# Expert results scattered by token, and the last layer's scores from rounded parts, in a two-layer attention and mixture-of-experts kernel

## The reference

```python
x = L0_attn_x
xn = _layernorm(x)
x = x + _L0_attn_ref(xn, ...) + _L0_ffn_ref(xn, Wg, W_in, W_out)
xn = _layernorm(x)
x = x + _L1_attn_ref(xn, key_param, ...) + _L1_ffn_ref(xn, gate_w, ...)

# _L0_attn_ref: causal attention, 16 heads of 16, 4 key heads, rotary
# _L0_ffn_ref: mixture of 8 experts with capacity C = 1280 each
top_vals, top_idx = jax.lax.top_k(softmax(xf @ Wg), 2)
loc = ...                      # place of the token in its expert's queue
keep = loc < C                 # what comes too late is dropped
gates = top_vals * keep / max(sum, 1e-09)
buf = zeros((E, C + 1, h)).at[e_flat, l_flat].set(xk)
a, g = split(einsum('ech,ehf->ecf', buf[:, :C], W_in), 2)
out_e = einsum('ecf,efh->ech', gelu(a) * g, W_out)
y = (out_pad[e_flat, l_flat].reshape(S, K, h) * gates[..., None]).sum(axis=1)

# _L1_attn_ref: queries against 32 learned patterns, sparsemax over them
scores = einsum('blhe,bshe->bhls', xn @ Wq + bq, keys)
out = einsum('bhls,bshd->blhd', sparsemax(scale * scores), values)
# _L1_ffn_ref: 8 experts and 2 shared ones, each over all tokens
```

## Time and profile before

| | us |
|---|---|
| Median of 3 runs | 2156.84 |
| Lowest and highest | 2152.84 and 2159.22 |
| The profiled execution | 2144.84 |
| Its span, first to last instruction | 2143.1 |
| TensorE busy | 1966.0 (92%) |
| VectorE busy | 1531.1 (71%) |
| ScalarE busy | 1035.6 (48%) |
| GpSimd busy | 514.3 (24%) |

### The profile page before, as it was taken

One profiled execution on the slowest core, in us unless ns is written; L12 is line 12 of the kernel. 1 busy time (PEld: TensorE's weight loads), 2 busy tenths in 40 slices (PEclk: granted clock), 3 DMA queues, 4 the chain that ended last, 5 costly groups with the idle time before them and its releaser, 6 DMA issues. The chain is left out here.

```text
span 2143.1 us, 35073 instructions
## 1 busy us (share of the span) xinstructions
PE 1966.0 (92%) x11874; PEld 1195.0 (56%) x11874; DVE 1531.1 (71%) x3473; ACT 1035.6 (48%) x2246; POOL 514.3 (24%) x932
## 2 busy tenths in 40 slices
PE   6869999999999999999799999986678999999998
PEld 3333333333333333333299999984556777777776
DVE  7879988888888888888054333325578998889883
ACT  3426677676767777777744444432331122221112
POOL 4554123322222222222233333336400000000000
PEclk9979999999999999999999999998789999999998
DMA  6555111111101111110133222215410000000005
GB/s 206 183 160 200 62 38 58 56 38 40 35 32 38 41 43 43 43 43 11 52 101 100 90 84 88 90 42 163 144 51 12 9 21 20 20 20 20 10 11 162
DMA packets 111781, 143.69 MB, mean 67 GB/s; under 512 B 12153, under 2 KB 96769, under 8 KB 111233
## 3 DMA queue, kind: packets, MB, share of 16 engines
q1 hardware_dynamic: 87248, 98.09, 14.3%
q0 software_dynamic: 10400, 31.47, 4.4%
q10 hardware_dynamic: 13968, 12.06, 1.8%
HBM read 85.10 MB, written 56.10 MB: 66 GB/s over the span
## 5 line engine op out<-in xcount | busy, mean ns | idle before, releaser
L854 ACT ACTIVATE at_wt<-at_B 128x512 f32<-128x512 f32 (+3 forms) x1280 | 607.3, 538 | 257.7 <-PE at_B L953 240.8
L1259 DVE TENSOR_REDUCE at_piece_max<-at_A 128x1 f32<-128x512 f32 x768 | 489.0, 684 | 71.3 <-PE at_A L934 61.8
L971 PE MATMUL at_O<-at_wt,at_v 128*32 128x512 f32 (+3 forms) x2560 | 313.9, 543 | 0.0
L754 POOL TENSOR_SCALAR_AFFINE_SELECT at_wt<-at_wt 128x128 f32<-128x128 f32 x512 | 147.8, 294 | 632.6 <-ACT at_wt L854 623.9
L1256 DVE CUSTOM_DVE_ANT_0 at_junk<-at_A,s_hide 128x128 bf16<-128x128 f32 (+3 forms) x512 | 230.5, 487 | 69.6 <-PE at_A L934 69.0
L1474 PE MATMUL ex_H<-ex_xT,ex_w_in 128*128 128x256 f32 x1920 | 247.8, 286 | 4.0 <-DVE ex_xT L1581 4.0
L1474 PEld LDWEIGHTS ex_H<-ex_xT,ex_w_in 128*128 128x128 f32 x1920 | 237.0, 193 | 4.4 <-DVE ex_w_out L1586 4.4
L1595 DVE TENSOR_TENSOR ex_h<-ex_act_a,ex_H 128x256 f32<-128x256 f32 x160 | 66.8, 417 | 212.7 <-ACT ex_act_a L1523 212.6
L2170 ACT ACTIVATE l_act_g<-l_G 128x512 f32<-128x512 f32 x80 | 47.9, 599 | 305.9 <-PE l_G L2084 241.3
L934 PE MATMUL at_A<-s_k,s_q 96*128 96x512 bf16 (+2 forms) x480 | 165.7, 363 | 22.3 <-PEq L104 9.6
L1516 POOL TENSOR_TENSOR ex_hT<-ex_h,ex_hT 128x256 fp32r<-128x256 f32 x160 | 123.1, 774 | 254.3 <-ACT ex_hT L1527 254.3
(11 more groups left out here) (275 smaller groups left out, 2798.9 us busy)
## 6 DMA issues: line engine op xcount, KB each, us to landing
buf<-at_room POOLq DMA_DIRECT2D x10, 1024.0 KB, 8.7
s_first_rows<-buf SPq DMA_DIRECT2D x40, 256.0 KB, 2.7
expert_out<-ex_y ACTq DMA_DIRECT2D x40, 256.0 KB, 2.2
s_raw_in<-in_W_in SPq DMA_DIRECT2D x8, 1024.0 KB
q_parts<-parts SPq DMA_DIRECT2D x16, 384.0 KB, 3.5
s_down<-in_x SPq DMA_DIRECT2D x8, 512.0 KB, 4.7
xn<-s_raw_in SPq DMA_DIRECT2D x8, 512.0 KB, 5.4
at_v<-v SPq DMA_DIRECT2D x16, 256.0 KB, 3.0
```

What stands on the lines that cost most here:

```text
L754: pool.affine_select(block_, block_, [[1, P]], ALU.is_ge, 0.0, base=0, channel_multiplier=-1).then_inc(hidden, 1)
L854: act.activation(wt[(HP * p + h) % NE_][:, q0:CH], pB_of(p, h, u)[:, q0:CH], ACT.Exp, scale=D ** -0.5).then_inc(wt_ready, 1)
L971: pe.matmul(pO[j % 2][rows, q0:CH], vs[n % 3][:, kt // TPC, kt % TPC, :], wt[(HP * p + h) % NE_][:, q0:CH], start=kt < 2 and not late, sto ...
L1259: ins = dve.tensor_reduce(top, pA[slot % NA][:, 0:w], AX.X, ALU.max)
```

## The change

Three things are changed together.

1. The experts' results. A slot's row in `buf` becomes 258 numbers long: the token's number in front, the index of its second expert behind. From these VectorE works out for each slot the row `token` or `4096 + token` (`find_target`), and GpSimd writes each step's result with two indirect DMAs of 128 rows to that row of `expert_out`, which now has 2 x 4096 rows in the order of tokens. Slots without a token carry a number beyond the bounds and are left out; `expert_out` is filled with zeros before. GpSimd does this behind the subtractions of f=1 and f=2 of the next step. `mixing` then loads `ye` with plain DMAs on SyncE.
2. The scores of the last layer. `to_scores` and the token columns are cut into two fp32r parts each, and a group takes six fp32r products instead of two float32 ones. The raw `to_scores` goes to HBM in the attention stage and comes back in mixing, where it is cut.
3. The loops of SyncE, GpSimd and VectorE in the experts and of VectorE in finish are written out. `mixed` is stored in two parts, the second over the attention output, and some semaphores are shared.

```diff
@@ attention: dispatch @@
+                if n == 0:
+                    pool.wait_ge(routing_in, 48)
+                    pool.tensor_copy(token[:, :, 1], expert[:, 1]).then_inc(token_set, 1)
+                    pool.wait_ge(token_set, 2)
...
                 for w in range(2):
-                    for c in (2 * n + w, TILES + 2 * n + w):
+                    pool.tensor_copy(xrow[n % 2][w][:, 0:E + 2:E + 1], token[:, 2 * n + w]).then_inc(token_set, 1)
+                for w in range(2):
+                    pool.wait_ge(token_set, 2 * n + w + 3)
+                    for k in range(TOPK):
+                        c = k * TILES + 2 * n + w
                         pool.indirect_dma_start(
...
+                    if n == 1 and p % 4 == 0 and p // 4 < NO_ROWS:
+                        pool.dma_start(no_rows[p // 4],
+                                       zeros[:, 1:E + 1].unsqueeze(1).to_broadcast([P, 8, E])).then_inc(buf_blank, 16)
...
+                if n == 0:
+                    sp.wait_ge(act_step, at_act["to_scores1"])
+                    sp.dma_start(d["scores_raw"], scores_raw[:]).then_inc(pats_in, 16)
@@ experts @@
-            with pool.Fori(0, ROUNDS) as j:
-                for i in range(PAIR):
-                    for f in range(FC):
-                        pool.wait_ge(h_high, FC * (PAIR * j + i) + f + 1)
-                        pool.tensor_tensor(hT[i % 2][1][:, f, :], h[i % 2][:, f, :],
-                                           hT[i % 2][0][:, f, :].bitcast(F32), ALU.subtract).then_inc(h_low, 1)
+            def store(m, t):
+                if t == 0:
+                    pool.wait_ge(target_ready, 2 * (m + 1))
+                    pool.wait_ge(y_ready, m + 1)
+                pool.indirect_dma_start(
+                    out=d["expert_out"], out_offset=bass.IndirectOffsetOnAxis(ap=target[m % 8][:, t:t + 1], axis=0),
+                    in_=y[m % 2][:, t, :], in_offset=None, bounds_check=TOPK * NT - 1, oob_is_err=False,
+                ).then_inc(y_stored[m % 2], 16)
+
+            for m in range(PAIR * ROUNDS):
+                for f in range(FC):
+                    pool.wait_ge(h_high, FC * m + f + 1)
+                    pool.tensor_tensor(hT[m % 2][1][:, f, :], h[m % 2][:, f, :],
+                                       hT[m % 2][0][:, f, :].bitcast(F32), ALU.subtract).then_inc(h_low, 1)
+                    if f in STORE_AT and m:
+                        store(m - 1, STORE_AT.index(f))
+            for t in range(RT):
+                store(PAIR * ROUNDS - 1, t)
...
-            def store(m, i):
-                act.wait_ge(y_ready, m + 1)
-                act.dma_start(one(rows_out, m), y[i][:]).then_inc(y_stored[i], 16)
...
+            def find_target(m, u):
+                dve.wait_ge(x_loaded[u % 2], 16 * (m // 2 + 1))
+                wait(dve, y_stored[u % 2], 16 * RT * (m // 2 - 3))
+                dve.tensor_scalar(second[u][:], x[u % 2][:, :, E + 1], float(m // PER), float(NT), ALU.is_equal,
+                                  ALU.mult).then_inc(target_ready, 1)
+                dve.wait_ge(target_ready, 2 * m + 1)
+                dve.tensor_tensor(target[u][:], second[u][:], x[u % 2][:, :, 0], ALU.add).then_inc(target_ready, 1)
...
+                        if f == 1 and not (last and i == PAIR - 1):
+                            find_target(m + 1, (m + 1) % 8)
@@ mixing @@
+                wait(sp, sums, SUMS * (t - NR + 1))
+                for k in range(TOPK):
+                    sp.dma_start(ye[k][t % NR][:], ye_rows[k][t]).then_inc(rows_in[t % NR], 16)
...
-        @block.gpsimd
-        def _(pool):
-            for t in range(STEPS):
-                wait(pool, sums, SUMS * (t - NR + 1))
-                for k in range(TOPK):
-                    for w in range(2):
-                        c = k * TILES + 2 * t + w
-                        pool.indirect_dma_start(
-                            out=ye[k][t % NR][:, w, :], out_offset=None, in_=d["expert_out"],
-                            in_offset=bass.IndirectOffsetOnAxis(ap=s["slot_get"][:, c:c + 1], axis=0),
-                        ).then_inc(rows_in[t % NR], 16)
...
+                if t == SPLIT_AT:
+                    act.wait_ge(raw_in, 16)
+                    act.copy(s["to_scores0"][:], scores_raw[:])
...
+                if t == SPLIT_AT + 1:
+                    dve.wait_ge(aT_ready, SPLIT_AT + 2)
+                    dve.tensor_tensor(s["to_scores1"][:], scores_raw[:], s["to_scores0"][:].bitcast(F32), ALU.subtract)
@@ layer1 @@
-                for k in range(EC):
-                    ins = pe.matmul(pZ[:], xT_score[:, k, t, :], s["to_scores"][:, k, :],
-                                    start=(k == 0), stop=(k == EC - 1))
+                steps = [(a, b, k) for a, b in TERMS for k in range(EC)]
+                for a, b, k in steps:
+                    ins = pe.matmul(pZ[:], xT_score[a][:, k, t, :], s[f"to_scores{b}"][:, k, :],
+                                    start=(a, b, k) == steps[0], stop=(a, b, k) == steps[-1])
...
-                for t in range(TPC):
-                    ins = act.copy(xT_score[:, k, t].rearrange("p (t r) -> p t r", r=16), cols[:, c % NQ * TPC + t])
-                ins.then_inc(score_cols, 1)
+                act.copy(score_view(0, k), score_rows(c, k)).then_inc(score_cols, 1)
...
+            def score_lows(c, k):
+                dve.wait_ge(score_cols, EC * c + k + 1)
+                dve.tensor_tensor(score_view(1, k), score_rows(c, k), score_view(0, k).bitcast(F32),
+                                  ALU.subtract).then_inc(score_low, 1)
...
+                    if c + 1 < NCH and i in SCORE_LOWS:
+                        score_lows(c + 1, SCORE_LOWS.index(i))
```

More of the change, by code:

```diff
@@ L533, in attention @@
         tile_count, tile_before = (scratch(KT * NX) for _ in range(2))
-        loc, within, drop, slot, slot_low, slot_put, kept = (scratch(KT) for _ in range(7))
-        FAR = float(1 << 20)
+        loc, within, drop, slot, slot_put, kept = (scratch(KT) for _ in range(6))
+        scores_raw = sb("scores_raw", [P, EC, H * NPAT])
         def half(i):
@@ L904, in _ @@
                 act.wait_ge(pe_step, at_pe[f"fold{k}"])
-                st.did(act.copy(columns(s["to_scores"][:, k], E), pQ))
+                st.did(act.copy(columns(scores_raw[:, k], E), pQ))
                 mlp_copy(4 + k)
@@ L1371, in experts @@
         y = [sb(f"y{i}", [P, RT, E]) for i in range(2)]
+        second = [sb(f"second{i}", [P, RT]) for i in range(8)]
+        target = [sb(f"target{i}", [P, RT], U32) for i in range(8)]
         over_sum = sb("over_sum", [P, TILES, H])
@@ L1452, in round_ @@
                         weights(2 * j + i // PER + 1)
-            with sp.Fori(0, ROUNDS - 1) as j:
-                round_(j, True)
-            round_(ROUNDS - 1, False)
+            for j in range(ROUNDS):
+                round_(j, j + 1 < ROUNDS)
         @block.tensor
@@ L1558, in round_ @@
                             keep(m - 1, 1 - b)
-                        if f == 2 and not (first and i == 0):
-                            store(m - 1, 1 - b)
                         if f == 2:
@@ L1572, in _ @@
             keep(PAIR * ROUNDS - 1, 1)
-            store(PAIR * ROUNDS - 1, 1)
-            for i in range(2):
-                act.wait_ge(y_stored[i], 16 * (PAIR // 2 * ROUNDS))
         @block.vector
@@ L1619, in _ @@
             xT_rest(0, 0)
-            round_(0, True, False)
-            with dve.Fori(1, ROUNDS - 1) as j:
-                round_(j, False, False)
-            round_(ROUNDS - 1, False, True)
+            find_target(0, 0)
+            for j in range(ROUNDS):
+                round_(j, j == 0, j == ROUNDS - 1)
 def mixing(nc, d, s):
@@ L1906, in layer1 @@
         MIX, SCORE, HIGH, LOW = 1, 6, 3, 4
[L1907 removed]
+        SCORE_LOWS = (2, 3)
+        seg = sb("seg", [P, TPC * ZW // 2], BF16)
         inv_k = sb("inv_k", [P, NPAT])
         xT = token_columns(s)
[L1910 removed]
+        xT_score = [sb(f"xT_score{a}", [P, EC, TPC, P], F32R) for a in range(2)]
         xp = [sb(f"xp{u}", [P, 2, EC, CH], F32R) for u in range(2)]
@@ L2332, in _ @@
             dve.memset(ones[:], 1.0).then_inc(ones_ready, 1)
+            for k in range(EC):
+                score_lows(0, k)
             pick()
@@ L2489, in _ @@
                 add(t, t)
-            with dve.Fori(1, ROUNDS - 1) as j:
+            for j in range(1, ROUNDS - 1):
                 for u in range(2):
@@ L2544, in build @@
             experts(nc, d, s)
+        for a in range(2):
+            keep(f"to_scores{a}", [P, EC, H * NPAT], F32R)
         keep("top", [P, TILES, 8])
```

109 lines of the change are left out of this document (64 added, 45 removed).

## The result

| | before | after |
|---|---|---|
| Median of 20 runs, us | 2158.03 | 2168.91 |
| Lowest and highest | 2145.35 and 2169.75 | 2164.81 and 2174.3 |
| Profiled execution | 2144.84 | 2167.05 |

The ratio is 1.006, with a 95% interval of 1.0047 to 1.0073: slower by 0.6%, about 11 us between the medians. The forecast was 2168 in 2134 to 2202. The number came out, and by luck: two errors of the account, of 11 and 10 us, cancel.

A forecast was written before the change was run, and what follows sets the result against it. TensorE was taken to bound the experts, TensorE and VectorE nearly the last layer, and no engine mixing. +41 + 2 - 33 + 1 + 0 = +11 us gave 2156 profiled, 2168 as median, range 2134 to 2202.

The forecast's parts named there:

- The standstill in mixing: Mixing: gathers replaced by plain loads, so the time in which TensorE's results are held goes; 33 us gained.
- rival B: Mixing: the hold on TensorE stays, as plain loads bring it too or its own queue does; 2201 us, chance 0.13.
- The stall in the experts: Experts: two scatters in GpSimd's chain start `output` 1.05 us late in each of 39 steps, +41 us.
- The room of 1.45 us: Experts: margin of 0.32 us plus GpSimd's idle time in the chain, into which a step's new work must fit.
- Rival A: Experts: scatters cost TensorE nothing, as the next subtraction may begin under one; 2127 us, chance 0.25.
- Between the stages: Experts to mixing: two scatters and a landing after the last step delay mixing's start, +2 us.
- Attention: Attention stage: more zero writes, a load, a store and small GpSimd copies are covered by waits, 0 us.
- Last layer: Last layer's scores: fp32r products gain 3.4 us, VectorE's added subtractions lose 4.2; taken as 0.
- The sum, and the median: Whole kernel: +11 us on the profiled 2144.84 gives 2156; 12 us from profiled execution to median carried over, 2168.
- Rival C: Experts: scatters hold TensorE as gathers do in mixing, or the granted clock falls; 2205 us, chance 0.12.

The follow-up runs named there:

- chips of the first kind: Three of the four experiment chips; the kernel before, unchanged, takes 2147 to 2150 us there.
- the quiet chip: One of the four experiment chips; the kernel before, unchanged, profiled once more there: 2097.93 us.
- late scatters: The changed kernel with both scatters of a step behind the subtraction of f=3: ratio to before 1.0057 and, on a chip where before takes 2146.92, 0.9844.
- the second chip: The changed kernel itself, run again on another chip: 2168.43 us against 2150.31 for the kernel before, ratio 1.0092.

## Why the number was right, point by point

**The standstill in mixing** (-33, bounds 0 and 35): right, -33.6. That the gathers hold TensorE's results was an inference from where the standstills were not. It is shown now from both sides, for chips of the first kind: without gathers no remote wait, with 64 idle ones 37.7 us more. On the quiet chip the same gathers cost 4.6 us. With plain loads of the same bytes at 200 GB/s there is no remote wait, so rival B falls. The rule of the Trainium skill that was weighed against the trace (SBUF — State Buffer, "Who interferes with whom": TensorE and ScalarE wait on nobody at SBUF) gave 0 and is not borne out as an account of this stage's time. What in a gather holds the results stays open. Whether it is the reading side, the descriptors or the semaphores was not tried, and the scatters of the experts, two per 10 us, don't do it visibly.

**The stall in the experts** (1.05 us a step, bounds 0.45 to 1.85): right in kind and nearly in size, 1.13 a step. The chain on GpSimd is what sets `output`. The room of 1.45 us was well read: one scatter fits and costs nothing, two don't. Rival A falls because the subtraction behind a scatter doesn't start under it: 1311.53 + 1.26 = 1312.79, and the subtraction starts at 1312.81. In the step shown the two scatters with all their gaps took 1.44 and 1.19 us, 2.63 together, where 2 x 1.31 = 2.62 was reckoned. But two of its parts were wrong and cancelled: the gap before a scatter was 0.15 to 0.17, not 0.30, and the first scatter took 1.26, not 1.01. That is so in the steps in which VectorE cuts weights beside it; 21 of the changed kernel's 80 scatters overlap such a cut and all take about 1.3 us, of the other 59 only 8 do. The step is 1.21 longer where the sum said 1.05, because `output` starts 0.05 behind the chain and the chain 0.09 later behind the last `output`. In steps without cuts it is only 0.92 longer: their chain was 2.87 us long before, not 3.47, so the one step that was read stood for two kinds. 39 x 1.13 makes 44.1, and the last step's extra wait with a fallen clock 3.1 more.

**Between the stages** (+2, bounds 0 and 9): mis-sized, +8.6. I added issue and landing, and took the landing to be the end. The trace's records show the landings of the last scatter at 1497.0 to 1497.2 and a drain of GpSimd from 1497.45 on, 6.59 us long. Taking the last scatters away gives 7.9 us back. The failed step is the term itself: it had no drain in it, though the kernel before shows one of 7.77 us at the end of attention. There the last scatter had ended at 1033.96, 27 us before the drain began, so the drain doesn't count from the last DMA. Wherever GpSimd had issued DMAs in a stage, its drain took over 5 us (6.4 to 6.6 at the end of the experts, 7.8 to 8.0 at the end of attention), and 0.8 to 1.6 in the latents and experts of the kernel before, where it had issued none. Which of its DMAs, plain or indirect, bring it, and what it waits for, isn't known.

**Attention** (0): wrong, +3.6 in the profiles and +10 on the quiet chip, where the dispatches blur it least. From ScalarE's first activation of the stage to the first expert product it is 921.8 there in the kernel before and 920.7 with plain loads in mixing, but 931.6 and 932.6 with both and with one scatter late. Some 3 of the 10 us lie before the first exponential, where the cause is open; the rest is lost before the 106th, where the fill runs. I had counted the bytes of the new writes, though four more of them where the page has eight (`expert_out`, x8), and the cover of the new copies. I had not asked what rows of 1032 bytes do to the fill of `buf`, which shares the queue time with the loads of the second head pair. The fill in whole pieces mends 5 us of it by the 106th exponential; at the end of attention 0.8 and, with late scatters, 3.5 were left on a chip of the first kind. On the quiet chip it didn't run, so how much of the 10 us it would mend there is not shown. The Trainium skill (DMA: Bandwidth & Descriptors, "How a descriptor splits into AXI transactions") says that a piece which doesn't start on a 256-byte boundary costs transactions whose bytes are partly thrown away. The trace agrees in direction, 236 GB/s at a share of 1.03 against 356 at 0.97, and with pieces of 8256 bytes the landing is 8.4 us again. Whether that splitting is the reason, no run here shows.

**Last layer** (0, bounds -6 and +6): right, -2.8 in the two profiles. Over all of them, kernels with the old last layer took 525.4 to 528.8 us, those with the new one 520.2 to 525.9. The scores don't explain the difference, since with the old products the stage took 523.9; what does is open.

**The sum, and the median.** The profiled executions differ by 22.2 us where the sum said 11: too little by 7 between the stages, 6 in the experts and 4 in attention, less 5 by which mixing, the last layer and finish came out better. Then I carried over the 12 us by which the first profiled execution was faster than its median. That step failed. The changed kernel has no such 12 us: its profiled execution lies 1.9 under its median, and its runs spread over 9.5 us against 24.4 before. The wide spread belongs to the kernel before; another of its kind (plain loads in mixing) reached the experts' first product at 1090.6 instead of 1077.3 in its profiled execution. From the first exponential to the last it took 902.0 us there and 887.8 in the first profile, and that execution was 9.5 us over its median. The difference lies at the dispatch's bursts: set against the quiet chip, they cost up to 3.6 us each there. So the two errors, 11 and 10 us, cancelled. On the second chip the ratio is 1.009, and by the estimate above the quiet chip would show a much larger loss (mixing wins 4 there, the losses stay). Attention alone varies enough to hold the 12 us; how much of them is in mixing stays open.

**Rival C** (scatters hold TensorE in the experts, or the clock falls): not borne out. The granted clock of the stretch is 1.00, and with late scatters the period is 9.07. What it said of the experts is true of the dispatch in attention on the first chip, where the bursts cost about 17 us in all.

## What to carry to other kernels

An idle engine has room only at certain places of a step: look for where it can be late without making anyone wait (here behind the last subtraction of a step: with both scatters there GpSimd still waits 2.40 us before the chain begins again) and put new work there, not between the links of a chain that another engine waits for. Moving two scatters by one place turned 1.009 of before into 0.984 on chips of one kind. Take the spread of the kernel before as a finding: if its profiled execution lies 12 us under its median, ask which stage varies, and whether the change removes that stage's cause. And read what each stage's end costs: a drain of 7.8 us in the trace of before would have priced the new one.

## What was not expected of the hardware

- Chips differ where GpSimd's gathers in mixing and its dispatch in attention run beside the other engines. Mixing with the same gathers took 95.6 us on one chip and 125.3 on another, attention from its first to its last exponential 870.9 and 887.8; the experts, without such DMAs in the kernel before, 365.0 and 364.3.
- GpSimd left the stage 8.2 us after its last scatter's instruction had ended, 7 us after the last landing. Its drain at the end of a stage took 6.4 to 8.0 us in experts and attention where it had issued DMAs, even with the last of them 27 us back, and 0.8 where it had issued none.
- While rows of 1032 bytes filled a buffer, the DMA engines, busy all the time (share 1.00 to 1.06), moved 217 to 277 GB/s; with pieces of 8256 bytes up to 367 at a share of 0.90.
- The best kernel found, with late scatters and the whole fill, takes 0.984 of the kernel before on a chip where that takes 2147. That can't be told from late scatters alone (0.984) nor from plain loads in mixing alone (0.983, rows in slot order). On the quiet chip even the kernel with late scatters is 0.6% slower than the kernel before, and the best one didn't run there, so no version is shown to beat both kernels on every chip.
